# Cross attention in a decoder kernel: the last batch's output product in rounded passes in a buffer of its own, and its first loads two heads sooner

## What is computed

```python
q = rmsnorm((hidden_states @ Wq).reshape(B, Sq, H, D), gq)           # H = 16 heads of D = 128
k = rmsnorm((encoder_hidden_states @ Wk).reshape(B, Skv, H, D), gk)
v = (encoder_hidden_states @ Wv).reshape(B, Skv, H, D)
attn = softmax(jnp.einsum('bqhd,bkhd->bhqk', q, k) * scale, axis=-1)
out = jnp.einsum('bhqk,bkhd->bqhd', attn, v).reshape(B, Sq, H * D)
x = layernorm(x + out @ Wo)                                          # Wo: 2048 x 512
x = layernorm(x + (silu(x @ lut[gate_idx].T) * (x @ lut[up_idx].T)) @ lut[down_idx].T)
```

## Time and profile before

| | us |
|---|---|
| three runs | 2727.56, 2734.78, 2736.85 |
| median | 2734.78 |
| the profiled execution's own time | 2728.88 |
| its span, first to last instruction | 2727.2 |
| PE busy | 2534.4 (93%) |
| DVE busy | 1944.2 (71%) |
| ACT busy | 1276.6 (47%) |

### The profile page before, as it was taken

How to read it: one execution, slowest core, us unless ns; L and a number is a source line. 1 busy time by engine, 2 the same in 40 slices (tenths; PEclk the granted TensorE clock), 3 DMA queues, 4 the chain that set the end, 5 groups by cost and what they waited for, 6 DMA issues and landing times.

```text
span 2727.2 us, 30212 instructions
## 1 busy us (share of the span) xinstructions
PE 2534.4 (93%) x9938; PEld 1675.5 (61%) x9938; DVE 1944.2 (71%) x3609; ACT 1276.6 (47%) x2404; POOL 729.6 (27%) x721
## 2 busy tenths in 40 slices
PE   6999999989779998899999999999999998999997
PEld 2343433434367754577777776777777773688886
DVE  4899999899975578677778787778788785231332
ACT  4464554645433311476746665566646663121111
POOL 1446455556411255221212121121121110000000
PEclk8999999999989999899999999999999999999999
DMA  4112111112320301232323322332332215100000
GB/s 153 54 48 85 51 67 62 56 39 77 116 101 32 124 16 43 108 112 101 139 82 120 109 100 68 100 101 82 102 115 93 78 47 190 51 31 1 31 16 16
DMA packets 81606, 212.51 MB, mean 78 GB/s; under 512 B 8998, under 2 KB 17446, under 8 KB 77356
## 3 DMA queue, kind: packets, MB, share of 16 engines
q1 hardware_dynamic: 73196, 180.88, 20.0%
q0 software_dynamic: 5472, 21.01, 2.0%
q10 hardware_dynamic: 2784, 8.72, 0.9%
HBM read 164.11 MB, written 46.47 MB: 77 GB/s over the span
## 4 chain that ended last, share of the span: by engine, by line
PE 53%; DVE 27%; ACT 8%; issue 8%; POOL 3%; DMA 1%; DVEq 0%; SPq 0%; POOLq 0%; ACTq 0%
PE bank L729 13%; PE bank L1094 10%; DVE h L1890 6%; DVE val L2174 3%; PE bank L1269 3%; PE bank L1270 3%; PE bank L1273 3%; ACT p L1662 3%; DVE val L2167 3%; PE bank L1180 2%; PE bank L944 2%; PE bank L945 2%; PE bank L1203 1%; PE bank L1298 1%; PE bank L1299 1%
## 5 line engine op out<-in xcount | busy, mean ns | idle before, releaser
L2479 POOL TENSOR_TENSOR h<-du,Bb 128x1024 f32<-128x1024 f32 x128 | 313.0, 2448 | 220.8 <-DVE h L1898 220.3
L1890 DVE TENSOR_TENSOR_SCAN h<-bank,h 128x512 f32<-128x512 f32 x256 | 299.7, 1206 | 28.2 <-ACT bank L1443 20.9
L1443 ACT ACTIVATE bank<-dt,A 128x512 f32<-128x512 f32 x256 | 175.1, 690 | 304.2 <-DVE h L1890 302.8
L1662 ACT ACTIVATE p<-bank,sm,rq 128x512 f32<-128x512 f32 x256 | 195.9, 775 | 173.1 <-DVE sm L2303 173.1
L2557 POOL TENSOR_TENSOR rq<-rq,mhalf 128x4 f32<-128x4 f32 x64 | 84.6, 1321 | 690.7 <-DVE rq L2249 690.7
L729 PE MATMUL bank<-pT,v 128*128 128x512 f32 x512 | 230.2, 592 | 0.8 <-ACT pT L1325 0.8
L1898 DVE TENSOR_TENSOR h<-h,Cb 128x1024 f32<-128x1024 f32 x128 | 197.4, 1542 | 6.5
L944 PE MATMUL bank<-h,ident 128*128 128x512 f32 x256 | 148.0, 661 | 53.5 <-DVE h L1898 53.0
L282 POOL TENSOR_SCALAR rstd<-mv 128x1 f32<-128x1 f32 x80 | 23.6, 295 | 647.7 <-DVE mv L276 647.4
L2433 DVE TENSOR_TENSOR h<-bank,sg 128x512 f32<-128x512 f32 (+1 forms) x44 | 30.4, 690 | 227.5 <-PE bank L1273 227.5
L2299 DVE TENSOR_REDUCE sm<-bank 128x1 f32<-128x512 f32 x256 | 164.1, 681 | 2.9 <-PE bank L1094 2.6
(11 more groups left out here) (273 smaller groups left out, 6104.2 us busy)
## 6 DMA issues: line engine op xcount, KB each, us to landing
wxq_s<-wq_dram SPq DMA_DIRECT2D x48, 512.0 KB, 4.0
Bb<-bc_dram SPq DMA_DIRECT2D x32, 512.0 KB, 3.6
Cb<-bc_dram SPq DMA_DIRECT2D x32, 512.0 KB, 3.7
x_dram<-xo POOLq DMA_DIRECT2D x16, 1024.0 KB, 4.8
woh<-in_Wo SPq DMA_DIRECT2D x64, 256.0 KB, 2.6
xc<-x_dram SPq DMA_DIRECT2D x12, 1024.0 KB, 5.5
wxv_s<-wkv_dram SPq DMA_DIRECT2D x12, 1024.0 KB, 5.0
wxk_s<-wkv_dram SPq DMA_DIRECT2D x12, 1024.0 KB, 7.8
```

The lines of the kernel that those rows point to most:

```text
L1443: act.activation(bank[2 + n][:, :], dt[:, c % 2, et, :], ACT.Exp, scale=A[:, et, 2 * w + n:2 * w + n + 1]).then_inc(dA_ready, 1)
L1662: act.activation(p4[:, t, :], bank[4 + t][:, :], ACT.Exp, bias=sm4[:, 4 + t:5 + t], scale=rq[:, hh % 2, 1, t:t + 1], accum_out=sm4[:, 8 + ...
L1890: dve.tensor_tensor_scan(h[:, s, n, :], bank[2 + n][:, :], h[:, s, n, :], 0.0, ALU.mult, ALU.add).then_inc(scanned, 1)
L2479: pool.tensor_tensor(h[:, G % HR, :, :], du[:, et:et + 1, :].to_broadcast([P, 2, S]), Bb[:, w % 2, :, :], ALU.mult).then_inc(dBu_ready, 1)
```

## The change

Three edits:

1. The last batch's product is rounded like the others. Its hi and lo tiles (o_hiL, o_loL, w_hiL, w_loL, 8 rows of D values in all) lie in the tail of wdn_hi, the last weights' place, which is first written in the fifth stage. `out_whole` is gone.
2. ACT's and DVE's orders in batch 3 are written anew: heads 0 and 1 are rounded around the last oT and split between the pairs of the look-up's last unit, head 2 comes behind y_turned, head 3 behind the first two slice loads, and heads 4 to 15 stand three to every two slices.
3. In every batch the loads of woh for heads 0 and 1 are issued at head 14, ahead of that head's other transfers on SP; in batch 3 the load of the next x too. `load_wo` now waits for o_split alone in batch 3 as well.

```diff
+        last_at = s5w.at + 4 * (KF1 * D - 8 * D)
         wdn_hi = s5w("wdn_hi", [P, KF1, D], F32R)
+        lasts = Space(nc, last_at)
+        o_hiL = lasts("o_hiL", [P, 2, S], F32R); o_loL = lasts("o_loL", [P, 2, S], F32R)
+        w_hiL = lasts("w_hiL", [P, 2, D], F32R); w_loL = lasts("w_loL", [P, 2, D], F32R)
...
                 def load_wo(c, hh):
-                    sp.wait_ge(o_split, START + min(after(c, XH, max(0, hh - 1)), (B - 1) * XH))
-                    if c == B - 1 and hh >= 2:
-                        sp.wait_ge(wo_used, START + after(c, XH - 1, hh - 1))
+                    sp.wait_ge(o_split, START + after(c, XH, max(0, hh - 1)))
                     sp.dma_start(woh[:, hh % 2, :], io["Wo"][hh * P:(hh + 1) * P, :]).then_inc(wo_loaded[hh % 2], 16)
...
+                            if hh == XH - 2:
+                                load_wo(c, 0)
+                                load_wo(c, 1)
+                                if c == B - 1 and stages >= 5:
+                                    load_chunk(4, 0, 0, rows_of)
                             if hh % 4 == (2 if c and hh < XH - 4 else 3):
                                 store_unit(n)
...
-                        if c == B - 1 and stages >= 5:
-                            load_chunk(4, 0, 0, rows_of)
                         n = FIRST[c] + sum(LUTS[c])
-                        for hh in range(2):
-                            load_wo(c, hh)
                         if c == B - 1:
                             store_unit(n - 1)
...
                         for hh in range(XH):
-                            out_whole(c, hh)
+                            out_rounded(c, hh)
...
                         if c == B - 1:
+                            round_out(0)
                             bring(oT[:, XH - 1, :], got(c, "o", XH - 1))
+                            round_out(1)
+                            for k in range(KD if stages >= 5 else 0):
+                                act.wait_ge(a_full, START + A0[4] + k + 1)
+                                bring(y_hi[:, k, :], bank[k][:, :])
+                            round_out(2)
...
                 load_slice(0)
                 load_slice(1)
-                y_turned(0)
+                round_out(3)
                 for j, (n, k) in enumerate(slices):
+                    round_out(4 + 3 * (j // 2) + j % 2)
                     act.wait_ge(slice_in[j % 2], START + 16 * (j // 2 + 1))
                     if j + 2 < len(slices):
                         load_slice(j + 2)
                     act.activation((wg_hi, wu_hi)[n][:, k, :], (wg, wu)[n][:, k, :], ACT.Copy).then_inc(w_rounded, 1)
+                    if j % 2:
+                        round_out(6 + 3 * (j // 2))
...
                                     second_pair(n + 1)
+                                    out_rest(0)
                                     third_pair(n + 1)
+                                    out_rest(1)
                                     fourth_pair(n + 1)
...
-                            split_weights()
+                            out_rest(2)
+                            out_rest(3)
+                            for j in range(2 * KD):
+                                out_rest(4 + 3 * (j // 2) + j % 2)
+                                split_slice(j)
+                                if j % 2:
+                                    out_rest(6 + 3 * (j // 2))
                             dve.wait_ge(v_full, START + V0[4])
                             y_rest(0)
```

More of the change, by code:

```diff
@@ L1189, in out_rounded @@
                     pe.wait_ge(o_split, START + after(c, XH, hh + 1))
+                    o_hi, o_lo, w_hi, w_lo = (o_hi3, o_lo3, w_hi3, w_lo3) if c < B - 1 else (o_hiL, o_loL, w_hiL, w_loL)
                     for t in range(NT):
                         tt = slice(t * P, (t + 1) * P)
-                        pe.matmul(bank[4 + t][:, :], o_hi3[:, hh % 2, tt], w_hi3[:, hh % 2, :], start=(hh == 0), stop=False)
-                        pe.matmul(bank[4 + t][:, :], o_hi3[:, hh % 2, tt], w_lo3[:, hh % 2, :], start=False, stop=False)
-                        m = pe.matmul(bank[4 + t][:, :], o_lo3[:, hh % 2, tt], w_hi3[:, hh % 2, :], start=False, stop=(hh == XH - 1))
+                        pe.matmul(bank[4 + t][:, :], o_hi[:, hh % 2, tt], w_hi[:, hh % 2, :], start=(hh == 0), stop=False)
+                        pe.matmul(bank[4 + t][:, :], o_hi[:, hh % 2, tt], w_lo[:, hh % 2, :], start=False, stop=False)
+                        m = pe.matmul(bank[4 + t][:, :], o_lo[:, hh % 2, tt], w_hi[:, hh % 2, :], start=False, stop=(hh == XH - 1))
                         if hh == XH - 1:
@@ L1198, in out_rounded @@
                         m.then_inc(wo_used, 1)
-                def out_whole(c, hh):
-                    pe.wait_ge(wo_loaded[hh % 2], START + 16 * after(c, XH // 2, hh // 2 + 1))
-                    for t in range(NT):
-                        m = pe.matmul(bank[4 + t][:, :], oT[:, hh, t * P:(t + 1) * P], woh[:, hh % 2, :],
-                                      start=(hh == 0), stop=(hh == XH - 1))
-                        if hh == XH - 1:
-                            m.then_inc(v_full, 1)
-                        elif t == NT - 1:
-                            m.then_inc(wo_used, 1)
                 keys(0, 0, range(NT))
@@ L1691, in round_out @@
                             act.wait_ge(a_done, evicted4(c, "o", hh))
-                            act.activation(o_hi3[:, hh % 2, :], oT[:, hh, :], ACT.Copy)
+                            o_hi, w_hi = (o_hi3, w_hi3) if c < B - 1 else (o_hiL, w_hiL)
+                            act.activation(o_hi[:, hh % 2, :], oT[:, hh, :], ACT.Copy)
                             if hh == 0:
                                 act.wait_ge(a_full, evicted4(c, "o", XH - 1))
-                            act.activation(w_hi3[:, hh % 2, :], woh[:, hh % 2, :], ACT.Copy).then_inc(o_rounded, 1)
+                            act.activation(w_hi[:, hh % 2, :], woh[:, hh % 2, :], ACT.Copy).then_inc(o_rounded, 1)
                         if c == 0:
@@ L2208, in fourth_pair, with split_slice @@
                     choose(s, idx[:, n % 2, :], 1, n, 18)
[L2210 to L2213 removed]
+                def split_slice(j):
+                    k = j % KD
+                    dve.wait_ge(w_rounded, START + j + 1)
+                    if j < KD:
                         dve.tensor_tensor(wg_lo[:, k, :], wg[:, k, :], wg_hi[:, k, :], ALU.subtract).then_inc(gate_split, 1)
[L2215 to L2216 removed]
+                    else:
                         dve.tensor_tensor(wu_lo[:, k, :], wu[:, k, :], wu_hi[:, k, :], ALU.subtract).then_inc(up_split, 1)
@@ L2281, in out_rest @@
                             dve.wait_ge(o_rounded, START + after(c, XH, hh + 1))
-                            dve.tensor_tensor(o_lo3[:, hh % 2, :], oT[:, hh, :], o_hi3[:, hh % 2, :], ALU.subtract)
-                            dve.tensor_tensor(w_lo3[:, hh % 2, :], woh[:, hh % 2, :], w_hi3[:, hh % 2, :], ALU.subtract).then_inc(o_split, 1)
+                            o_hi, o_lo, w_hi, w_lo = (o_hi3, o_lo3, w_hi3, w_lo3) if c < B - 1 else (o_hiL, o_loL, w_hiL, w_loL)
+                            dve.tensor_tensor(o_lo[:, hh % 2, :], oT[:, hh, :], o_hi[:, hh % 2, :], ALU.subtract)
+                            dve.tensor_tensor(w_lo[:, hh % 2, :], woh[:, hh % 2, :], w_hi[:, hh % 2, :], ALU.subtract).then_inc(o_split, 1)
                         if c == 0:
```

5 lines of the change are left out of this document (removed).

## The result

| | before | after |
|---|---|---|
| median, us | 2729.93 (2727.56 to 2736.85, 5 runs) | 2709.8 (2706.97 to 2715.52, 5 runs) |
| the profiled execution's own time | 2728.88 | 2708.54 |
| its span | 2727.2 | 2706.9 |

The ratio is 0.9919 with an interval of 0.9903 to 0.9936: the change made the kernel 20 us faster (0.8%). The forecast was 2722.3, with a range down to 2714: the direction was right, the gain was forecast at 12.5 us and the range missed it by 4.2. The forecast was counted from a median of three runs, 2734.78; over five runs the kernel before has 2729.93. The changed kernel was measured beside the one before twice more, with ratios of 0.9929 [0.9911, 0.9946] and 0.995 [0.9934, 0.9966]: by the three ratios the gain is 14 to 22 us.

What follows compares the result with a forecast made beforehand. The last batch's product was taken as bound first by loads of woh sharing the DMA engines, then by PE. Gains of 8.9 us there and 3.7 in earlier batches, taken as 12.5, gave 2722.3 from 2734.78; range 2714 to 2733.

Steps and rivals of the forecast that it cites:

- The start: Last batch's product up to product 2: it starts at 2285.8, 5.3 us behind the kernel before, with PE idle 7.5 us.
- the store's chain: Ahead of product 2, head 2's load waits on SP behind the last unit's store, itself 2.6 us later behind DVE's fourth pair.
- The loop from head 2: Last product: ten heads at 3.3 us, then three at 2.75, ending at 2330.1 against 2339.03, 8.9 us won.
- The ring's formula: Last product's buffer, reloaded every two heads: (load's landing time + 2.6) / 2 us a head, beside PE's 2.72.
- The term L: Landing time of a woh load in the last product: 2.6 us without company, 5.2 with two slices in flight, taken as 3.9.
- rival 2: Last product PE bound from head 2 on, if slices rarely meet a load: 18.5 us won, 2716.3; chance 0.12.
- Rival 3: Products 2 to 15 slowed by a 1.2 GHz clock after PE's waits, 5.4 us a head; all slow 2753.5; chance 0.06.
- Earlier batches: Batches 0 to 2: first w_hi comes 1.4, 1.3 and 1.1 us sooner and the whole batch moves, 3.7 us won.
- Rival 4: Earlier loads in batches 0 to 2 do nothing, DVE's look-up taking up the 3.7 us: 8.9 won, 2725.9; chance 0.12.
- What moved behind: Loads of wdn, now issued behind head 15's rounding, cost nothing, covered by gate and up tiles; uncovered, up to 3 us.

Runs made afterwards that it cites:

- experiment 4: The changed kernel with the load of the next x put back behind head 15's store: 2715.52 us, ratio 0.9936 to the kernel before.
- experiment 9: The changed kernel with 512 KB more loaded beside each of the eight slices: 2722.27 us, ratio 0.9969 to the kernel before.
- experiment 8: The changed kernel with turn5's 16 transposes done three times more on PE before product 2: 2713.67 us, ratio 0.9938 to the kernel before.
- experiment 1: The kernel before with only the earlier loads of woh for heads 0 and 1 and the next x: 2726.52 us, ratio 0.9975 to the kernel before.
- experiment 3: The changed kernel with batches 0 to 2's loads of woh for heads 0 and 1 back behind head 15's store: 2718.94 us, ratio 0.9948.
- experiment 2: The changed kernel with loads of woh for heads 0 and 1 and next x back behind head 15's store in all batches: 2718.33 us, ratio 0.9946.

## Why the prediction was wrong

**Where the 20.3 us between the two profiled spans lie:** last part 12.2, batches 0 to 2 7.1 (gaps 2.1, heads 5.7, products 0.7 longer), stages ahead 1.6, batch 3's heads 0.1, and 0.7 lost behind.

**The start: right.** Product 2 began 12.5 us after product 0 (13.5 by the times forecast), with PE idle 6.45 us for w_lo (7.5), as the store's chain said. Counted from the last exponential it came 25.7 us after, 26.9 forecast: the load behind the store took 2.98 us instead of 3.56. No wait for xc, as forecast, and experiment 4 shows that it wouldn't have mattered.

**The loop from head 2: the step that failed.** The ring's formula held (experiment 9). The term L, the landing of woh while slices fly, was mis-sized: "I take the middle, L = 3.9 and 3.3 us a head", between ends of 2.6 and 5.2. It measured 2.6, the lower end, for which the same formula gives 2.6 us a head, below PE's own; heads 3 to 12 followed every 2.85 us on the mean. Over ten heads that is 4.5 us. It was rival 2's course, "PE bound from head 2 on", at 0.12. The middle of two bounds was no reading of a row. The 70% of DMA time that I worked out myself (65% measured) came near; what I did not ask is what a load meets. With two slices per three heads, each landing in 4.2 us, only the loads of heads 4 and 5 flew beside two slices issued together (3.8 and 5.2 us). Each load from head 6 on went out 2.4 us or more behind the last slice's issue, met one slice, or parts of two, or none, and took 2.5 to 2.9. The distance between the two issues matters: in the 11 profiles with a rounded last product and slices of the usual size, the 7 loads of woh that were issued less than 1 us behind a slice took 4.6 to 7.3 us to land, and the 60 that were issued over 2.2 us behind the last one, with one slice in flight, 2.7 in the median (2.5 to 5.0). No experiment moved this distance alone. It did not come out as evenly in the two further profiles of the change: single loads behind head 6 took up to 4.7 us, and heads 3 to 15 followed every 2.91 and 3.00 us instead of 2.84, still well below 3.3.

**The clock: a term left out.** Product 2 at a granted 0.52 was 2.4 us longer than forecast. Rival 3 had the place right and the extent wrong: one head of fourteen, none behind the short waits. From the last exponential on: 8.9 forecast + 1.2 (start) + 4.5 (pace) - 2.4 (clock) = 12.2, as measured. In experiment 8 taking this term away won 1.3 us by product 4 and lost more at product 6.

**Earlier batches: half right.** Of 3.7 us the gaps gave 1.8 to 2.1 (experiments 1 and 3, and the counts over 17 profiles). "I expect the whole batch to move": it moved by 0.6 to 0.9 us a batch in the first pair of profiles. The first w_hi did come as soon as forecast (1963.68, right behind the last weighted head). But w_lo was done at 1965.63, and PE began at 1966.20, having had work of its own until then (the turned x, L1138, in the rows above). Before, w_lo (done at 1975.85) and PE's own work both ended just ahead of the product's start at 1976.00, since PE had stood idle for oT, which ACT brings behind the late roundings: 0.70, 0.62 and 0.40 us in the three gaps, 1.7 in all, against 0.15 after. There was hardly more to win. I had asked whether DVE would take the gain up, not how long PE stood idle: a wait that is taken away is worth about the idle time that it leaves on the engine behind it. The further 4 to 6 us in the heads go with a lower granted clock (0.98 against 0.99 in batch 2); I couldn't tie them to the change. Rival 4 (the earlier loads do nothing) fell, by 2 us.

**What moved behind: nearly nothing, as said.** ACT waited for no wdn. The rest is 0.7 us longer in all profiles with a rounded last product (388.8 or 388.9 against 388.1); 0.35 of it lie between the product and the first down product. The other half was not traced.

**The sum:** 18 us for the change in the stages that it touches, of which 13.7 can be tied to its edits (12.6 + 1.8 - 0.7), against 12.5 forecast. That these two are so near is in part luck: the last part won 3.7 us more than its 8.9, the gaps 1.9 less than their 3.7. In the first comparison the 3.3 us of the last product alone would not have left the range. The rest was in no term: 4 to 6 us of heads with a higher clock, 1.6 of stages ahead, and the point from which I counted. The median before fell by 4.9 us, from 2734.78 over three runs to 2729.93 over five; a range laid from there would have begun at about 2709.1, just under the 2709.8 measured. Two us for scatter between runs was too little for a kernel whose untouched stages differ by 8.7 us among six profiles.

**Slips in the working.** The loads between the two of the earlier trace rows were not "alike": they took 4.6 to 5.3 us, which is the 5.2 that the loop was then reckoned with. 27.77 us for eight heads are 3.47 a head, not 3.43, which is the step from one start to the next. The chances add up to 0.61 faster and 0.33 the same. None of these moves the forecast by 1 us.

## What to carry to other kernels

When a loop is a ring of load, round and multiply, work out the pace from each end of the load's time and ask which end the new order of the issues brings about; if one end lies below the engine's own pace, that engine is the likely bound, and the middle is a forecast of neither. Close a gap only together with what stands behind it: here neither the loads of two heads ahead nor a full clock won anything alone, and by the traces the loads brought 1.6 and then 4.4 us once the roundings behind the slices were moved as well. Before giving a gain of under 1%, cut two profiles of the same kernel into its stages, and let the range take in what the untouched ones scatter.

## What the runs showed of the hardware

- A load of 256 KB landed in 2.6 us beside slices that were issued at intervals (DMA 65% busy, 219 GB/s), in 4.5 us with 512 KB more per slice, in 5.2 us beside two slices always in flight (92%, 313 GB/s), and in 6.5 us where two of them shared the engines with a load of 1 MB (experiment 2). These are medians.
- A load of 256 KB issued less than 1 us behind one of 688 KB took 4.6 to 7.3 us (7 loads in 11 profiles); issued over 2.2 us behind it, 2.7 in the median (60 loads, 2.5 to 5.0).
- Behind an idle of 6.45 us of PE the granted clock was 0.52 for 5.15 us; behind one of 3.27 us (experiment 1) 0.71 over 10 us; behind one of 2.40 us (experiment 8) 0.63 over 4.4 us, and behind one of 2.00 us before 0.64 over 4.8; behind one of 1.71 us 1.00. But behind the 3.62 us of the earlier trace rows 16 matmuls took 7.03 us, the length at 1.00. The full clock over product 2 did not shorten the stretch (experiment 8: 72.3 us against 69.0): the load of head 6 then took 5.66 us instead of 2.49.
- In heads whose instructions are the same, PE was busy for 3.1 us more in one profile than in another, at a granted 0.98 instead of 0.99, with 4.2 us of idle time in either. Over 17 profiles three batches' heads took 665 to 671 us. The first three stages, which no edit touches, took 1132.7 to 1151.4; PE was busy there for 1001.8 us at a granted 0.95 in the shortest and for 1021.8 at 0.94 in the longest.
